# GpSimd subtracts for every second table, constants in the comparisons, and another order at the end, in an embedding lookup and MLP kernel

## The chip, the core and the metric

The kernel runs on one core of a Trainium2 chip. The core has a matrix engine (TensorE, PE in the profile, with its weight loads as PEld), three engines for elementwise work (VectorE = DVE, ScalarE = ACT, GpSimd = POOL) and SyncE (SP), which here only starts DMAs. They run side by side and wait for one another by semaphores. The metric is the device time of one execution, in microseconds (us), as a median over runs.

## What is computed

```python
e = stack([tbl_f[ids[:, f]] for f in range(32)], axis=1)      # (2048, 32, 64)
gram = einsum('bnd,bmd->bnm', e, e)
z = gram[:, rows, cols]                                        # 496 pairs above the diagonal
h = concatenate([z, dense_ctx], axis=1)                        # (2048, 512), dense_ctx has 16 columns
h = maximum(h @ W_top1 + b_top1, 0.0)                          # 512 -> 512
h = maximum(h @ W_top2 + b_top2, 0.0)                          # 512 -> 256
y = h @ W_top3                                                 # 256 -> 1
```

All is float32. 9 tables have 1000 rows, 8 have 1250, the rest 12500 or 125000.

## The kernel before

**Tiling.** The batch of 2048 is cut into eight super tiles of 256 examples (`SUPERS`, s = 0 to 7). The 17 smallest tables are `LOOKED_UP` (unit u = 0 to 16): their rows are not gathered but picked by matrix products. The other 15 tables are gathered by GpSimd with indirect DMAs (L264), two per table and super tile, so 30 in each super tile and 240 in all.

**A lookup by products.** A table lies in SBUF over 125 partitions, with 8 rows of it in each partition (1000 rows, u = 0 to 8) or 10 (1250 rows, u = 9 to 16); this number is `SPAN[u]`. VectorE makes one 0/1 matrix for each of the SPAN rows (`make_onehot`, L575): it compares `place`, the id of each example, spread over all partitions, with the partition's own code, a float32 per partition read from `codes_sb`. PE multiplies the 0/1 matrices with the table (`look_up`, L329), 2 x SPAN products for one unit. To keep float32's precision with bfloat16 products, each table is held in `split_sb` as three bfloat16 parts: high, middle and low.

**The head.** These parts are made once, while super tile 0 is looked up. For each unit ScalarE makes the high part (`high`, L504), VectorE subtracts it from the table (`take_high`, L605, into one of two `residue` buffers), ScalarE makes the middle part (`middle`, L508) and VectorE subtracts again to make the low part (`low`, L610). The semaphore `table_split` counts the low parts: PE waits for it ahead of each lookup of super tile 0, and `take_high` of the unit two further on waits for it because of the buffer. VectorE's order in the head is fixed in code: comparisons of u, `take_high(u+1)`, `low(u)`. The ids of super tiles 0 and 1 are spread over the partitions by PE in five pieces (`PIECES`, `spread_ids`, L315) and copied to `place` by ScalarE (`place_ids`, L476); those of later super tiles come by DMA. PE does a few products of no use before each lookup (`stay_warm`, L382). GpSimd does nothing but gathers: those of super tile 0 and then, when the index array has landed, those of super tile 1 and on; from super tile 2 on a gather waits for the drain that frees its rows.

**The middle.** In `step(s)` PE transposes the 32 fields in 8 groups (`transpose_group`, L299 and L302), computes the pair products (`gram_batch`, L346), and between these looks up super tile s+1 and does the MLP of s-1 (L358, L368, L375). The results of the pair products are folded by ScalarE (L463) and VectorE (L560) and laid out anew by 16 SBUF-to-SBUF DMAs (`move_cells`, L205); then 4 small DMAs write the 16 dense columns into `pairs` (L236), over cells that a move has written before.

**The end.** `step(7)` has nothing to look up. Its transposes go through four PSUM banks, drained by ScalarE and VectorE in turn (L441). Before its last group PE does 32 products of no use (`WARM_LAST`). Then come the pair products of s = 7, layers 1 to 3 of s = 6, and, once the 16 moves (10 from SP's queue, 6 from GpSimd's) and the 4 dense DMAs of s = 7 have landed, layers 1 to 3 of s = 7.

Of the kernel before, what the change touches and what calls it, by code (L numbers as in the profile page):

```python
# [9 lines left out]
P = 128  # L10
TILES = 2
# [5 lines left out]
WARM_FIRST, WARM_NEXT, WARM_LAST = 12, 4, 32  # L17
# [20 lines left out]
TP = 125  # L38
# [7 lines left out]
PIECES = [(0, 4), (4, 8), (8, 12), (12, 16), (16, 17)]  # L46
PIECE_OF = [p for p, (a, b) in enumerate(PIECES) for _ in range(a, b)]
assert len(PIECE_OF) == UNITS == FIRST_UNITS
# [8 lines left out]
READY_MADE = 3  # L57
assert READY_MADE < RING and READY_MADE <= UNITS
SP_MOVES = 10
# [34 lines left out]
def build(nc, ids, tables, dense, w1, b1, w2, b2, w3, identity, second, looked_ids, codes, out):  # L94
# [5 lines left out]
    with ctx:  # L100
# [44 lines left out]
        residue = [h1[0:TP].rearrange("p o b -> p (o b)"), pairs[0:TP, 0].rearrange("p i j q -> p (i j q)")]  # L145
# [24 lines left out]
        moved_by_pool = sem("moved_by_pool")  # L170
        dense_placed = [sem("dense_placed_even"), sem("dense_placed_odd")]
# [7 lines left out]
        whole_loaded = [sem(f"whole_loaded_{u}") for u in range(UNITS)]  # L179
        codes_loaded = sem("codes_loaded")  # L180
# [12 lines left out]
        table_split = sem("table_split")  # L193
# [13 lines left out]

        @block.sync
        def _(sp):
            sp.dma_start(index[:, 0], ids_v[0]).then_inc(first_index_loaded, 16)  # L210
            sp.dma_start(whole_ids, looked_ids).then_inc(whole_ids_loaded, 16)
            sp.dma_start(codes_sb[:], codes).then_inc(codes_loaded, 16)
# [9 lines left out]
            sp.dma_start(second_sb[:], second).then_inc(second_loaded, 16)  # L222
            for to, of in ((w1_sb, w1), (b1_sb, b1), (w2_sb, w2), (b2_sb, b2), (w3_sb, w3)):
                sp.dma_start(to[:], of).then_inc(weights_loaded, 16)

            def rearrange_pairs(s, parity, own=len(MOVES)):
# [5 lines left out]
                sp.wait_ge(pairs_moved, 16 * (len(MOVES) * s + own))  # L232
                if own < len(MOVES):
                    sp.wait_ge(moved_by_pool, 16 * (len(MOVES) - own))
# [432 lines left out]
```

## Time and profile before

| | us |
|---|---|
| median of 3 runs | 423.11 (422.06 to 423.18) |
| the profiled execution, its own time | 422.19 |
| its span in the trace | 420.4 |
| PE busy | 391.7 (93%) |
| VectorE busy | 297.6 (71%) |
| GpSimd busy | 249.3 (59%) |
| ScalarE busy | 168.9 (40%) |

All times in the trace count from the start of the span. The 1.8 us between the span and the execution's own time lie around the span and are not traced. A record's length is not the distance to the next one: VectorE's and PE's records overlap a little, so where a rate is wanted it is read from one start to the next. "Idle before" names what ended an engine's wait.

### The profile page before, as it was taken

The numbers are of one execution on the slowest core, as the hardware profiler recorded it, in microseconds if no ns is written. First come the engines' busy times: TensorE is split into PE (matmuls) and PEld (weight loads), VectorE is DVE, ScalarE is ACT, GpSimd is POOL, SyncE is SP. The second block draws the span as 40 slices with busy tenths as digits, with TensorE's granted clock in tenths as the row PEclk, the third lists the DMA queues.
The fourth block names the chain that finished last, engine by engine and source line by source line (L and its number), as shares of the span: only waits on it lengthen the run. The fifth ranks groups of instructions, "written<-read, shape, count | busy, mean of one in ns | idle before, by whom it ended". The sixth has DMA issues, their size and how long they took to land.

```text
span 420.4 us, 13473 instructions
## 1 busy us (share of the span) xinstructions
PE 391.7 (93%) x5554; PEld 357.0 (85%) x5554; DVE 297.6 (71%) x1295; ACT 168.9 (40%) x323; POOL 249.3 (59%) x250
## 2 busy tenths in 40 slices
PE   0876878999999999999999999999999999999987
PEld 0665668998999899988999899989999899989865
DVE  0799999998998379954998199846996389503200
ACT  2766743533533244323532354324532353222212
POOL 5777687777777777777777747774677700000200
PEclk9999999999999999999999999999999999999999
DMA  4445515212241342122511241132212200010100
GB/s 109 142 146 156 205 36 105 56 28 45 62 119 42 77 83 76 28 57 55 125 29 41 67 109 38 28 72 56 91 30 48 56 2 3 13 42 4 42 13 1
DMA packets 20991, 26.63 MB, mean 63 GB/s; under 512 B 9542, under 2 KB 13862, under 8 KB 20051
## 3 DMA queue, kind: packets, MB, share of 16 engines
q1 hardware_dynamic: 12882, 17.62, 12.5%
q0 software_dynamic: 7872, 8.08, 12.3%
q8 instruction: 44, 0.72, 0.8%
q14 instruction: 17, 0.14, 0.1%
q10 hardware_dynamic: 176, 0.08, 0.1%
HBM read 21.46 MB, written 0.08 MB: 51 GB/s over the span
## 4 chain that ended last, share of the span: by engine, by line
PE 81%; DVE 10%; DMA 3%; SPq 2%; issue 2%; ACT 2%; DVEq 0%
PE turn_ps L329 43%; PE mlp_ps L358 12%; PE gram_ps L346 8%; DVE onehot L575 6%; PE mlp_ps L368 6%; PE mlp_ps L299 5%; PE mlp_ps L302 3%; DVE split_sb L610 3%; PE mlp_ps L375 2%; DMA id_row<-half_ids 1%; SPq L205 1%; PE gram_ps L382 1%; ACT place L476 1%; PE mlp_ps L382 1%; DMA index<-looked_ids 1%
## 5 line engine op out<-in xcount | busy, mean ns | idle before, releaser
L264 POOL DMA_INDIRECT rows<-tbl,index x240 | 246.1, 1026 | 88.5 <-issue 71.6
L575 DVE TENSOR_SCALAR onehot<-place,codes_sb 125x256 bf16<-125x256 f16 x1216 | 250.9, 297 | 8.4 <-PE turn_ps L329 5.0
L329 PE MATMUL turn_ps<-split_sb,onehot 125*128 125x192 bf16 x2432 | 219.0, 246 | 10.7 <-DVE split_sb L610 10.7
L329 PEld LDWEIGHTS turn_ps<-split_sb,onehot 125*128 125x128 bf16 x2432 | 199.7, 98 | 17.2 <-DVE split_sb L610 14.0
L470 ACT CAST parts<-turn_ps 128x384 bf16<-128x384 f32 x136 | 65.2, 480 | 125.3 <-PE turn_ps L329 123.8
L553 DVE COPY y_room<-mlp_ps 1x256 f32<-1x256 f32 x8 | 5.0, 627 | 78.8 <-PE mlp_ps L375 78.8
L358 PE MATMUL mlp_ps<-pairs,w_sb 128*128 128x256 f32 x256 | 56.9, 380 | 1.0 <-DMA pairs<-dense 1.0
L358 PEld LDWEIGHTS mlp_ps<-pairs,w_sb 128*128 128x128 f32 x256 | 48.0, 190 | 7.8 <-DMA pairs<-dense 1.5
L441 ACT COPY emb_t<-mlp_ps 128x512 f32<-128x512 f32 x58 | 34.0, 586 | 14.3 <-PE mlp_ps L299 13.4
L346 PE MATMUL gram_ps<-emb_t 64*64 64x64 f32 x2048 | 37.5, 221 | 1.2 <-DVE folded L560 0.7
L346 PEld LDWEIGHTS gram_ps<-emb_t 64*64 64x64 f32 x2048 | 33.3, 134 | 6.1 <-issue 6.1
L205 POOL DMA_DIRECT2D pairs<-folded x6 | 3.0, 520 | 59.3 <-DVE folded L560 59.3
L560 DVE COPY_PREDICATED folded<-second_sb,gram_ps 128x512 f32<-128x512 int32 x32 | 23.1, 721 | 19.3 <-ACT folded L463 19.3
L458 ACT ACTIVATE h<-mlp_ps,b_sb 128x256 f32<-128x256 f32 x32 | 13.4, 471 | 47.5 <-PE mlp_ps L358 41.5
L463 ACT COPY folded<-gram_ps 128x512 f32<-128x512 f32 x32 | 18.8, 586 | 28.7 <-PE gram_ps L346 27.4
L299 PE MATMUL mlp_ps<-ident_bf,parts 128*128 128x128 bf16 x384 | 27.7, 219 | 1.4 <-ACT ident_bf L533 0.8
L368 PE MATMUL mlp_ps<-h,w_sb 128*128 128x256 f32 x128 | 28.9, 379 | 0.0
L299 PEld LDWEIGHTS mlp_ps<-ident_bf,parts 128*128 128x128 bf16 x384 | 23.5, 98 | 4.6 <-ACT parts L470 2.6
L368 PEld LDWEIGHTS mlp_ps<-h,w_sb 128*128 128x128 f32 x128 | 23.9, 190 | 3.7
L315 PE MATMUL gram_ps<-id_row,ones 1*125 1x512 f16 (+1 forms) x18 | 7.3, 508 | 10.7 <-DMA id_row<-half_ids 9.6
L302 PE MATMUL mlp_ps<-ident_sb,rows 128*128 128x128 f32 x112 | 17.1, 272 | 0.0
L482 ACT ACTIVATE h<-mlp_ps,b_sb 128x256 f32<-128x256 f32 x16 | 6.7, 471 | 20.9 <-PE mlp_ps L368 20.9
(37 smaller groups left out, 123.6 us busy)
## 6 DMA issues: line engine op xcount, KB each, us to landing
place<-ids_scratch SPq DMA_DIRECT2D x6, 1062.5 KB
pairs<-folded SPq DMA_DIRECT2D x122, 32.0 KB
rows<-tbl,index POOLq DMA_INDIRECT x240, 3.8
emb_t<-tbl SPq DMA_DIRECT2D x8, 250.0 KB
folded<-tbl SPq DMA_DIRECT2D x5, 312.5 KB
w_sb<-w SPq DMA_DIRECT2D x1, 1024.0 KB
y_room<-tbl SPq DMA_DIRECT2D x3, 312.5 KB
w_sb<-w SPq DMA_DIRECT2D x1, 512.0 KB
```

The lines of the kernel that those rows point to most:

```text
L264: nc.gpsimd.indirect_dma_start(rows[:, s % 2, slot - UNITS, t, :], None, tables[f][:, :], bass.IndirectOffsetOnAxis(index[:, s, t, f:f + 1 ...
L299: last = nc.tensor.matmul(turn_bank[g % banks][:, k, :], parts[:, slot, a].rearrange("p t d -> p (t d)"), ident_bf[:], start=(a == 0), sto ...
L302: last = nc.tensor.transpose(turn_bank[g % banks][:, k, :], rows[:, parity, slot - UNITS].rearrange("p t d -> p (t d)"), ident_sb[:])
L329: last = nc.tensor.matmul(turn_ps[:, n % 2].rearrange("p k b -> p (k b)")[:, t * PARTS * DIM:(t + 1) * PARTS * DIM], onehot[:, n % RING, c ...
L346: last = nc.tensor.matmul(gram_ps[FIELDS * i:FIELDS * (i + SIDE), k % 2, t, u].rearrange("p h ij -> p (h ij)"), e.rearrange("p b f -> p (b ...
L358: last = nc.tensor.matmul(mlp_ps[:, o // 2, o % 2, :], w1_sb[:, jj, P * o:P * (o + 1)], pairs[:, parity, :, jj, :], start=(jj == 0), stop= ...
L368: last = nc.tensor.matmul(mlp_ps[:, 0, o, :], w2_sb[:, k, P * o:P * (o + 1)], h1[:, k, :], start=(k == 0), stop=(k == OT1 - 1))
L441: copy(emb_t[:, :, GROUP_F * g:GROUP_F * (g + 1)], turn_bank[g % banks].rearrange("p f b -> p b f")).then_inc(done, 1)
L463: nc.scalar.copy(folded[:, parity, :, :, BATCH_Q * k:BATCH_Q * (k + 1)].rearrange("p i j (q t) -> p (i j) q t", t=TILES), gram_ps[:, k % 2 ...
L470: nc.scalar.copy(parts[:, u], turn_ps[:, n % 2].rearrange("p k b -> p (k b)")[:, 0:TILES * PARTS * DIM] .rearrange("p (t a d) -> p a t d", ...
L560: nc.vector.copy_predicated(folded[:, parity, :, :, BATCH_Q * k:BATCH_Q * (k + 1)].rearrange("p i j (q t) -> p (i j) q t", t=TILES), secon ...
L575: last = nc.vector.tensor_scalar(onehot[:, n % RING, c, :], place[:, parity, u, :], codes_sb[:, CODE_AT[SPAN[u]] + c:CODE_AT[SPAN[u]] + c ...
```

## The change

1. **Head, low parts.** `low(u)` of even u (0, 2, ... 16: nine units) is issued by GpSimd instead of VectorE, in its queue behind gathers 9, 12, 15, ... 33, counted from 0 (`LOW_BEHIND`). `table_split` becomes two semaphores, for even and for odd units. A third residue buffer is added, so `take_high(u)` waits for the low part of u-3 instead of u-2.
2. **Comparisons.** For s = 0 and 1 the code is a constant in the instruction instead of a float32 per partition from `codes_sb`. For this `place_ids` subtracts SPAN x partition from the ids by a per-partition bias (`shift_sb`, a new small DMA ahead of those of codes, identity and tables), and `PIECES` is cut so that no piece mixes the two spans.
3. **End.** The four tiles of layer 1 of s = 6 are issued before the last transpose group in the place of the 32 warm products. The transposes of `step(7)` use two banks instead of four (the other two now belong to layer 1). The 16 moves of s = 7 are issued 6 by SP, 5 by ScalarE and 5 by GpSimd. The dense columns of s = 7 are loaded early into `last_dense` (1 mask DMA and 4 data DMAs on SP, ahead of the weights) and put in place by one masked VectorE copy of 1024 elements per partition, in the place of the 4 DMAs behind the moves.

```diff
-PIECES = [(0, 4), (4, 8), (8, 12), (12, 16), (16, 17)]
+PIECES = [(0, 4), (4, 8), (8, 9), (9, 13), (13, 17)]
+LOW_BEHIND = [9 + 3 * n for n in range((UNITS + 1) // 2)]
-SP_MOVES = 10
+SP_MOVES, ACT_MOVES = 6, 5
...
         @block.gpsimd
         def _(pool):
+            def low(u):
+                pool.wait_ge(middle_split, u + 1)
+                nc.gpsimd.tensor_tensor(part(u, 2), table_rows(u, residue[u % len(residue)]), part(u, 1),
+                                        ALU.subtract).then_inc(table_split[0], 1)
...
                         ).then_inc(rows_landed[s % 2][slot // GROUP_F], 16)
+                        made = (FIELDS - UNITS) * TILES * s + TILES * (slot - UNITS) + t
+                        if made in LOW_BEHIND:
+                            low(2 * LOW_BEHIND.index(made))
...
                 if first:
-                    pe.wait_ge(table_split, u + 1)
+                    pe.wait_ge(table_split[u % 2], u // 2 + 1)
...
                     if not ahead and g == GROUPS - 1:
+                        for o in range(OT1):
+                            layer1_tile(s - 1, o, 1 - parity, turn - 1 + parity)
                         pe.wait_ge(second_copied, GRAM_EMPTY + GRAM_BATCHES * s)
-                        stay_warm(WARM_LAST, last_warm)
-                    transpose_group(s, parity, turn, g, 2 if ahead else 4)
+                    transpose_group(s, parity, turn, g, turn_bank if ahead else last_bank)
...
-                nc.scalar.copy(place[:, s, a:b, :].rearrange("p u q -> p (u q)"),
-                               gram_flat[0:TP, piece % 2, 0:SUPER * (b - a)]).then_inc(placed, 1)
+                nc.scalar.activation(place[:, s, a:b, :].rearrange("p u q -> p (u q)"),
+                                     gram_flat[0:TP, piece % 2, 0:SUPER * (b - a)], ACT.Identity,
+                                     bias=shift_sb[:, piece:piece + 1]).then_inc(placed, 1)
...
                     last = nc.vector.tensor_scalar(onehot[:, n % RING, c, :], place[:, parity, u, :],
-                                                   codes_sb[:, CODE_AT[SPAN[u]] + c:CODE_AT[SPAN[u]] + c + 1], None, ALU.is_equal)
+                                                   codes_sb[:, CODE_AT[SPAN[u]] + c:CODE_AT[SPAN[u]] + c + 1]
+                                                   if s > 1 else float(c), None, ALU.is_equal)
...
             def take_high(u):
-                if u >= 2:
-                    dve.wait_ge(table_split, u - 1)
+                if u >= len(residue):
+                    v = u - len(residue)
+                    dve.wait_ge(table_split[v % 2], v // 2 + 1)
...
                 if u + 1 < UNITS:
                     take_high(u + 1)
-                low(u)
+                if u % 2:
+                    low(u)
...
+            nc.vector.copy_predicated(pairs[:, 1].rearrange("p i j q -> p j i q"),
+                                      dense_mask[:].unsqueeze(2).unsqueeze(2).to_broadcast([P, CHUNKS, QUAD, QUADS]),
+                                      last_dense[:].unsqueeze(1).to_broadcast([P, CHUNKS, QUAD, QUADS])
+                                      ).then_inc(last_dense_placed, 1)
             layer3_drain(SUPERS - 2)
             layer3_drain(SUPERS - 1)
```

GpSimd's queue before, whole: the gathers follow one another without anything between them.

```order
6 L264 DMA rows<-tbl,index 128x64 x240
7 L205 DMA pairs<-folded 32x256 x6
8 L100 UNCONDITIONAL_BRANCH
```

GpSimd's queue now, the head part of it: ten gathers, then an instruction named ISA that the kernel's code does not ask for (the build puts it in front of the first subtraction), then nine subtractions with three gathers between each two.

```order
6 L293 DMA rows<-tbl,index 128x64 x10
7 L284 ISA
8 L284 TENSOR_TENSOR split_sb<-h,split_sb 125x8x64
9 L293 DMA rows<-tbl,index 128x64 x3
10 L284 TENSOR_TENSOR split_sb<-pairs,split_sb 125x8x64
11 L293 DMA rows<-tbl,index 128x64 x3
...
24 L284 TENSOR_TENSOR split_sb<-pairs,split_sb 125x10x64
25 L293 DMA rows<-tbl,index 128x64 x206
```

So every low part of an even unit now stands behind that ISA instruction and behind the gathers ahead of it.

PE at the end, before (L382 are the products of no use, L346 the pair products, L358, L368 and L375 the layers 1 to 3, first of s = 6, then of s = 7):

```order
244 L302 MATMUL mlp_ps<-ident_sb,rows 128x128 x7
245 L302 MATMUL turn_ps<-ident_sb,rows 128x128 x4
246 L382 MATMUL gram_ps<-ident_sb 128x128 x32
247 L302 MATMUL turn_ps<-ident_sb,rows 128x128 x4
248 L382 MATMUL gram_ps<-ident_sb 128x128 x4
249 L346 MATMUL gram_ps<-emb_t 64x64 x128
250 L358 MATMUL mlp_ps<-pairs,w_sb 128x256 x16
251 L368 MATMUL mlp_ps<-h,w_sb 128x256 x8
252 L375 MATMUL mlp_ps<-h,w_sb 1x256 x2
253 L358 MATMUL mlp_ps<-pairs,w_sb 128x256 x16
```

PE at the end, now (the same functions stand at L334, L416, L378, L392, L402 and L409):

```order
243 L334 MATMUL turn_ps<-ident_sb,rows 128x128 x11
244 L392 MATMUL mlp_ps<-pairs,w_sb 128x256 x16
245 L334 MATMUL turn_ps<-ident_sb,rows 128x128 x4
246 L416 MATMUL gram_ps<-ident_sb 128x128 x4
247 L378 MATMUL gram_ps<-emb_t 64x64 x128
248 L402 MATMUL mlp_ps<-h,w_sb 128x256 x8
249 L409 MATMUL mlp_ps<-h,w_sb 1x256 x2
250 L392 MATMUL mlp_ps<-pairs,w_sb 128x256 x16
```

Layer 1 of s = 6 has moved from behind the pair products to before the last transpose group, where the 32 products of no use were.

## Rows read from the trace of the kernel before

**Rows 1.** The page's chain that ended last, by engine:
```profile
PE 81%; DVE 10%; DMA 3%; SPq 2%; issue 2%; ACT 2%; DVEq 0%
```
**Rows 2.** Windows (us, busy us of each engine, granted clock): head, step 0, end:
```profile
18.00:65.00 47.00, 36.29 (x359) 30.51 (x358) 46.09 (x165) 29.30 (x50) 35.31 (x31) 1.00 0.41 132
65.00:111.00 46.00, 44.57 (x762) 43.20 (x761) 44.18 (x208) 19.60 (x39) 35.02 (x37) 1.00 0.29 62
```
**Rows 3.** Timeline (start, us) of one unit in the head, all engines:
```profile
57.09 0.81 DVE L605 TENSOR_TENSOR pairs<-y_room,split_sb 125x640 f32<-125x640 f32 x1
57.58 1.88 POOL L264 DMA_INDIRECT rows<-tbl,index  x1 [0.30 <-issue]
57.83 0.81 DVE L610 TENSOR_TENSOR split_sb<-h,split_sb 125x640 bf16<-125x640 f32 x1
58.56 2.20 DVE L575 TENSOR_SCALAR onehot<-place,codes_sb 125x256 bf16<-125x256 f16 x10
58.70 1.82 PE L329 MATMUL turn_ps<-split_sb,onehot 125*128 125x192 bf16 x20 [1.17 <-DVE split_sb L610]
59.77 0.94 POOL L264 DMA_INDIRECT rows<-tbl,index  x1 [0.30 <-issue]
60.36 0.60 PE L382 MATMUL mlp_ps<-ident_sb 128*128 128x128 f32 x4
60.53 0.81 DVE L605 TENSOR_TENSOR h<-y_room,split_sb 125x640 f32<-125x640 f32 x1
```
**Rows 4.** Timeline: the first lookup, the longest gather and gather 10, the last lookup:
```profile
13.21 2.27 POOL L264 DMA_INDIRECT rows<-tbl,index  x1 [0.30 <-issue]
17.03 1.23 POOL L264 DMA_INDIRECT rows<-tbl,index  x1 [0.30 <-issue]
17.69 1.77 PE L329 MATMUL turn_ps<-split_sb,onehot 125*128 125x192 bf16 x16
...
64.84 1.82 PE L329 MATMUL turn_ps<-split_sb,onehot 125*128 125x192 bf16 x20 [0.44 <-DVE split_sb L610]
```
**Rows 5.** Groups by shape (busy us, mean ns of one): ScalarE's copies, a subtraction:
```profile
L470 ACT CAST parts<-turn_ps 128x384 bf16<-128x384 f32 x136 | 65.2, 480 | 125.3 <-PE turn_ps L329 123.8 <-issue 1.5
L441 ACT COPY emb_t<-mlp_ps 128x512 f32<-128x512 f32 x58 | 34.0, 586 | 14.3 <-PE mlp_ps L299 13.4 <-PE mlp_ps L302 0.6 <-issue 0.2
L458 ACT ACTIVATE h<-mlp_ps,b_sb 128x256 f32<-128x256 f32 x32 | 13.4, 471 | 47.5 <-PE mlp_ps L358 41.5 <-issue 6.0
L610 DVE TENSOR_TENSOR split_sb<-h,split_sb 125x512 bf16<-125x512 f32 x5 | 3.4, 682 | 0.9 <-ACT split_sb L508 0.9
L511 ACT ACT_TABLE_LOAD x1 | 1.3, 1283 | 0.8 <-PEq L637 0.8
```
**Rows 6.** The comparisons' line: duration in ns, min/median/max, first and last start:
```profile
L575 DVE TENSOR_SCALAR onehot<-place,codes_sb x1216: 246/280/524, 11.8 to 362.2; 125x256 bf16<-125x256 f16 x174
```
**Rows 7.** DMA issues: KB each, us from issue to landing:
```profile
ids_scratch<-half_ids ACTq DMA_DIRECT2D x1, 68.0 KB, 5.7
id_row<-half_ids SPq DMA_DIRECT2D x1, 8.5 KB, 13.5
```
**Rows 8.** Groups in the window 13 to 66 us, GpSimd alone:
```profile
L264 POOL DMA_INDIRECT rows<-tbl,index x34 | 41.0, 1207 | 12.9 <-issue 10.1 <-DMA index<-ids 2.9
```
**Rows 9.** Timeline of the end:
```profile
382.40 3.66 PE L382 MATMUL gram_ps<-ident_sb 128*128 128x128 f32 x32
...
392.51 7.17 PE L358 MATMUL mlp_ps<-pairs,w_sb 128*128 128x256 f32 x32
...
393.34 0.73 DVE L560 COPY_PREDICATED folded<-second_sb,gram_ps 128x512 f32<-128x512 int32 x1 [0.20 <-ACT folded L463]
394.10 6.28 SPq L205 DMA_DIRECT2D pairs<-folded  x10
...
401.69 2.78 SPq L236 DMA_DIRECT2D pairs<-dense  x4
...
405.71 7.17 PE L358 MATMUL mlp_ps<-pairs,w_sb 128*128 128x256 f32 x32 [0.99 <-DMA pairs<-dense]
```

More of the change, by code:

```diff
@@ L16 @@
 QUADS = SUPER // QUAD
[L17 removed]
+WARM_FIRST, WARM_NEXT = 12, 4
 SIDE = 2
@@ L44 @@
 RING = 4
-PIECES = [(0, 4), (4, 8), (8, 12), (12, 16), (16, 17)]
+PIECES = [(0, 4), (4, 8), (8, 9), (9, 13), (13, 17)]
 PIECE_OF = [p for p, (a, b) in enumerate(PIECES) for _ in range(a, b)]
-assert len(PIECE_OF) == UNITS == FIRST_UNITS
+assert len(PIECE_OF) == UNITS == FIRST_UNITS and all(len(set(SPAN[a:b])) == 1 for a, b in PIECES)
 SPANS = sorted(set(SPAN))
@@ L91, in slot_meaning, with build @@
     return rows, np.tile(second, (QUAD, SIDE))
-def build(nc, ids, tables, dense, w1, b1, w2, b2, w3, identity, second, looked_ids, codes, out):
+def build(nc, ids, tables, dense, w1, b1, w2, b2, w3, identity, second, dense_cells, looked_ids, codes, shift, out):
     fp32, i32, bf16, fp16 = mybir.dt.float32, mybir.dt.int32, mybir.dt.bfloat16, mybir.dt.float16
@@ L206, in move_cells, with part, table_rows @@
                                     folded[FIELDS * i:FIELDS * (i + 1), parity, i % SIDE, CHUNKS * jq:CHUNKS * (jq + 1), :])
+        def part(u, which):
+            return split_sb[:, SPAN_AT[u]:SPAN_AT[u + 1], which, :]
+        def table_rows(u, flat):
+            return flat[:, 0:SPAN[u] * DIM].rearrange("p (c d) -> p c d", d=DIM)
         @block.sync
@@ L230, in rearrange_pairs @@
                     move_cells(sp, i, jq, parity).then_inc(pairs_moved, 16)
-                sp.wait_ge(pairs_moved, 16 * (len(MOVES) * s + own))
-                if own < len(MOVES):
-                    sp.wait_ge(moved_by_pool, 16 * (len(MOVES) - own))
+                if not place_dense:
+                    return
+                sp.wait_ge(pairs_moved, 16 * len(MOVES) * (s + 1))
                 for jj in range(CHUNKS):
@@ L441, in drain_turned @@
             copy(emb_t[:, :, GROUP_F * g:GROUP_F * (g + 1)],
-                 turn_bank[g % banks].rearrange("p f b -> p b f")).then_inc(done, 1)
-        def part(u, which):
-            return split_sb[:, SPAN_AT[u]:SPAN_AT[u + 1], which, :]
-        def table_rows(u, flat):
-            return flat[:, 0:SPAN[u] * DIM].rearrange("p (c d) -> p c d", d=DIM)
+                 banks[g % 2].rearrange("p f b -> p b f")).then_inc(done, 1)
         @block.scalar
@@ L489, in step @@
                             keep_parts(s + 1, u)
-                    drain_turned(act, nc.scalar.copy, turned_drained, s, g, 2 if ahead else 4)
+                    drain_turned(act, nc.scalar.copy, turned_drained, s, g, turn_bank if ahead else last_bank)
+                if not ahead:
+                    layer1_half(s - 1, 0)
+                    layer1_half(s - 1, 1)
                 for k in range(SLOTS):
@@ L507, in middle @@
                 act.wait_ge(high_taken, u + 1)
-                nc.scalar.copy(part(u, 1), table_rows(u, residue[u % 2])).then_inc(middle_split, 1)
+                nc.scalar.copy(part(u, 1), table_rows(u, residue[u % len(residue)])).then_inc(middle_split, 1)
             act.wait_ge(whole_ids_loaded, 16)
@@ L664 @@
     out = nc.dram_tensor("out", (BATCH, 1), mybir.dt.float32, kind="ExternalOutput").ap()
-    build(nc, ids, tables, dense, w1, b1, w2, b2, w3, identity, second, looked_ids, codes, out)
+    build(nc, ids, tables, dense, w1, b1, w2, b2, w3, identity, second, dense_cells, looked_ids, codes, shift, out)
     return run_bass_kernel_spmd(nc, [arrays], core_ids=[0]).results[0]["out"]
```

84 lines of the change are left out of this document (58 added, 26 removed).

## The prediction

> **What bounds the kernel now.** I read the chain that ended last first: 81% of it is PE, 10% VectorE [rows 1]. The windows say where VectorE's part lies. In the head (18 to 65 us) VectorE is busy 46.09 of 47 us and PE 36.29; in step 0 PE is busy 44.57 of 46 [rows 2], and from there to the last super tile PE has no gap worth naming. The granted clock is 1.00 in both stretches [rows 2], the upper level of 2.4 GHz. So time can come from two places: the head, which VectorE sets, and the end, where PE waits for the dense DMAs. In the head the timeline of one unit shows the pace [rows 3]: from `take_high` at 57.09 to the next at 60.53 is 3.44 us, made of two subtractions (57.09, 57.83, 58.56: 0.74 us each) and ten comparisons (58.56 to 60.53: 0.197 each). PE waits 1.17 us for the low part in each such unit. The first lookup runs at 17.69, the last at 64.84 [rows 4]: the head is these 47.2 us.
>
> **The comparisons (part 2).** In the head 9 x 8 + 8 x 10 = 152 comparisons lose their per-partition scalar. What that is worth no row shows; it is bounded from both sides. A subtraction of 512 elements takes 682 ns [rows 5] and one of 640 takes 0.81 us [rows 3]: about 1.02 ns per element, so some 0.16 us of a record are fixed. A comparison of 256 elements takes 280 ns in the median [rows 6]. If it streams two elements per such step, it takes 0.13 + 0.16 = 0.29 and the scalar costs nothing: the one end, 0. If it streams four, 0.065 + 0.16 = 0.225 and the scalar costs about 0.06. ScalarE is the other end: its copies of 384 and 512 elements take 480 and 586 ns, so one of 256 would take 374, and an activation of 256 with a per-partition bias takes 471 [rows 5], 0.10 us more. I take 0.06, the value that VectorE's own rows give if the scalar costs anything. That makes a comparison 0.14 and VectorE's head shorter by 152 x 0.06 = 9.1 us, if nothing else comes late. In step 0 the same saving falls beside a busy PE [rows 2] and is worth nothing. `place_ids` pays ScalarE's 0.1 us ten times, on an engine that is busy 29 of 47 us [rows 2].
>
> **The low parts (part 1).** VectorE gives up nine subtractions, five of 0.60 us (from start to start, 512 elements) and four of 0.74: 5.9 us. GpSimd gets them, and there they stand in one queue with the gathers. Three costs follow.
>
> First, the ISA instruction that the order shows between gather 9 and the first subtraction. No row of the trace has one. Its lower end is 0. It brings something in that this engine did not need before, so the nearest rows are those of loads: ScalarE's table load takes 1.28 us [rows 5], a DMA of 68 KB issued at 4.79 us on a queue of its own, with the table loads under way, lands after 5.7 us, and one queued behind the tables after 13.5, the upper end [rows 7]. I take a fetch and an installation, 5.7 + 1.3 = 7.0 us. The Trainium skill ("GPSIMD Engine Reference", § 2.1 Instruction dispatch) says that the first call to a freshly loaded GpSimd kernel pays about 6 us that the profile does not show as an instruction; no run here shows it yet. By that figure the sum below would be 1 us less, and it speaks against this change as a whole.
>
> Second, a subtraction on GpSimd. Lower end: VectorE's 0.68 us [rows 5]; upper end: the longest thing that GpSimd does in the head, a gather of 2.27 us [rows 4]. I take 1.2 for 512 elements and 1.4 for 640, in the lower half, since it moves two streams as VectorE does but in software. The same page (§ 3) gives 4497 ns for 2048 elements, in proportion an estimate of 1.1 and 1.4.
>
> Third, the pace of the queue. A gather takes 0.94 us and 0.30 of issue ahead of it [rows 3], 1.24 in all, but it is stretched while VectorE subtracts: 1.88 us for the one that meets two subtractions [rows 3]. Over the head 34 gathers average 1.207 us [rows 8], 0.267 more than 0.94, together 9.1 us for 33 subtractions, 0.28 each.
>
> Now the head after the change. Gather 10 began at 17.03 [rows 4]; in its place stands the ISA instruction, until 24.0. `low(0)` is done at 25.3 and PE looks unit 0 up at 25.4 instead of 17.7. VectorE meanwhile prepares units 1 to 3 and stops at `take_high(3)`, which waits for that low part. From `low(0)` to `low(16)` GpSimd has to do 24 gathers (24 x 1.24 = 29.8), eight subtractions with their waits (4 x 1.3 + 4 x 1.5 = 11.2) and the stretching by the 21 subtractions that VectorE has left (21 x 0.28 = 5.9): 46.9 us. The others are faster. VectorE has 128 comparisons (17.9), 14 `take_high` and 7 `low` (14.3) left, 32 us. PE's records are 1.77 us for 16 products, 1.82 for 20 and 0.60 for four warm ones [rows 3, 4]; they overlap, so 9 x 2.37 + 8 x 2.42 = 40.7 us and some 3 for the id pieces are more than it needs. So GpSimd sets the pace of the head and the 9.1 us of the comparisons are covered by its queue. The last lookup comes at 25.4 + 46.9 = 72.3 instead of 64.84: **+7.4 us**. What waits behind GpSimd's waits: gathers 10 to 29 of super tile 0, needed by step 0's transposes some 10 us after the head, and the index load, for which gather 30 waits 2.9 us now [rows 8], is by then long there; both are hidden.
>
> **The end (part 3).** Before, from the last fold (393.34 + 0.73 = 394.07) to layer 1 of s = 7 at 405.71 there are 11.6 us: ten issues in 6.28, 1.3 to landing, four dense issues in 2.78 from 401.69, and 1.2 to landing [rows 9]. Now: six issues at 0.63 (3.8), landing 1.3, the masked copy. This one has 1024 elements per partition; the fold does 512 in 0.73 [rows 9], so its bounds are 0.73 and 1.46, and with 512 x 1.02 ns more I take 1.25. With 0.15 for the handovers that is 6.5: -5.1 us. ScalarE's and GpSimd's five issues each take less than SP's six. Layer 2 and 3 of s = 6 (3.6 + 1.0 and ScalarE's work behind its five issues) end some 2 us before that and are hidden. Against it stand two costs ahead of the pair products. Layer 1 (7.17 for its 32 records) takes the place of the warm products (3.66) [rows 9]: +3.5. With two banks a transpose group waits for the drain of the one two before it: 0.73 of transposes, 0.59 of ScalarE's copy [rows 5] and some 0.2 of handover per two groups, where four banks let PE run on: about +0.8 by the seventh group. Sum: **-0.8 us**. The five early dense and mask DMAs and the shift DMA cost 0.4 to 0.6 us of SP's time each, ahead of tables and weights; the only table that is waited for is the first, and 0.4 us there disappears in the wait for the ISA instruction.
>
> **Sum.** +7.4 - 0.8 = +6.6 us on the profiled execution's 422.19: 428.8. That execution lies 0.9 below the median of three runs, so I say 429.0. About 1.3 us (0.3%) is what a measurement here can tell from no change.
>
> **The rivals.**
> - *The ISA instruction is free or nearly* (chance 0.24). For it: no trace shows a price, and something may be resident. Then `low(0)` is done at 18.3, just behind PE's readiness at 17.7, GpSimd's 46.9 us end at 65.3 (+0.5), and the end gives 0.8: 421.9. This is the other side: its price decides, and the sign turns at about 0.3 us. With shorter subtractions or less stretching (5 us at most) this goes down to 417.
> - *GpSimd keeps up* (0.08). The load costs 7 us, but gathers are not stretched as before, because VectorE subtracts less densely; VectorE or PE then sets the pace. GpSimd without stretching needs 41 us: last lookup at 66.4, +1.6 - 0.8, so 423.0.
> - *The scalar costs nothing* (0.09). VectorE then needs 25.2 + 14.3 = 39.5 us after `low(0)`, which alone is still hidden. But if a subtraction on GpSimd keeps VectorE from working for its whole length, 10.4 us more come on top, and 50 us are more than GpSimd's 46.9: +3.1, so 432. The Trainium skill ("SBUF — State Buffer", § Who interferes with whom) says just this of the shared port pair, an exclusive lock that fully blocks the loser; in the trace a gather is stretched by subtractions [rows 3], while VectorE shows no such loss to gathers.
> - *The end turns round* (0.07). If SP's and ScalarE's issues share one generator, 11 issues at 0.63 take 6.9 instead of 3.8: +3.1, so 432.
> - The forecast itself, 425 to 431.5 with the load between 4 and 9.5 us: 0.52.
>
> That the comparisons or moves are not changed as described is excluded by the order of instructions. Whether PE's clock falls in the 7.7 us without a lookup no row shows; the first lookups would be slower for it, behind GpSimd's queue, and I add nothing.
>
> **Numbers.** Range 420.5 to 433.5: it holds the forecast's cases, the middle of the free-load case and both dear ones. Faster by over 0.3%: 0.13 of the first rival and 0.01 of the second, 0.14. Within 0.3%: 0.09 + 0.03, 0.12. Slower: 0.74.
>
> **What the profile after would show.** The first lookup (L361) near 25.4 us instead of 17.7, with a gap on GpSimd of about 7 us after its tenth gather: the load. The last one near 72. PE in the head waiting for GpSimd's `split_sb` of even units, not for VectorE; VectorE waiting in `take_high`; comparisons 0.14 us apart there and 0.20 later. GpSimd's subtractions at 1.2 and 1.4 us. From the last fold to the last layer 1, 6.5 us instead of 11.6, and 4.3 us more between the last lookup of s = 7 and the pair products. I am wrong if GpSimd shows no gap, if even units' low parts are ready before PE asks, or if layer 1 of s = 7 waits for moves issued by ScalarE.

## The result, and the profile after

The changed kernel takes **432.1 us** (median of 427.8 to 433.2), the one before 422.7 beside it: a ratio of 1.0205 [1.0128, 1.0281], 9.4 us slower. The profiled execution takes 433.18 us with a span of 431.4, against 422.19 and 420.4.

Where its 11.0 us lie, from one start to the next: the last lookup of the head begins at 73.40 instead of 64.84 [rows 4], **+8.56**. From there to the first transposes of s = 7 (386.82) there are 313.42 us, before 313.37: the middle is as it was. From there to the end of the last product (428.91) there are 42.09, before 39.71 (378.21 to 417.92): **+2.38**.

Windows of the kernel after (us, busy us of each engine, granted clock), against [rows 2]:

```profile
18.00:40.00 22.00, 17.22 (x172) 15.46 (x172) 19.91 (x70) 12.41 (x24) 17.51 (x17) 1.00 0.44 146
40.00:60.00 20.00, 16.56 (x128) 13.09 (x126) 16.11 (x68) 13.15 (x21) 14.92 (x10) 0.83 0.44 136
60.00:75.00 15.00, 9.21 (x85) 8.71 (x82) 8.27 (x47) 3.73 (x7) 12.14 (x7) 0.77 0.29 72
```

VectorE, which was idle for only 0.9 of 47 us in the head, now is for a fifth of 40 to 60 us and for almost half of 60 to 75, and PE's granted clock, 1.00 everywhere before, is 0.83 and 0.77.

GpSimd around its first subtraction, and the first lookup (timeline of after: start, duration), against [rows 4]:

```profile
14.39 0.94 POOL L293 DMA_INDIRECT rows<-tbl,index  x1 [0.31 <-issue]
15.43 1.18 POOL L284 TENSOR_TENSOR split_sb<-h,split_sb 125x512 bf16<-125x512 f32 x1
18.21 2.43 PE L361 MATMUL turn_ps<-split_sb,onehot 125*128 125x192 bf16 x16
```

The gather ends at 15.33, the subtraction starts 0.10 us later: the ISA instruction between them costs nothing that can be seen.

The other places, in order of time:

```profile
26.59 2.70 DVE L613 TENSOR_SCALAR onehot<-place 125x256 bf16<-125x256 f16 x8
26.91 1.16 POOL L284 TENSOR_TENSOR split_sb<-pairs,split_sb 125x512 bf16<-125x512 f32 x1
...
42.68 1.43 DVE L613 TENSOR_SCALAR onehot<-place 125x256 bf16<-125x256 f16 x10
43.24 4.95 POOL L284 TENSOR_TENSOR split_sb<-pairs,split_sb 125x640 bf16<-125x640 f32 x1 [1.27 <-ACT split_sb L542]
44.03 0.81 DVE L645 TENSOR_TENSOR pairs<-folded,split_sb 125x640 f32<-125x640 f32 x1
44.77 1.43 DVE L613 TENSOR_SCALAR onehot<-place 125x256 bf16<-125x256 f16 x10
46.12 0.81 DVE L645 TENSOR_TENSOR h<-folded,split_sb 125x640 f32<-125x640 f32 x1
47.00 1.87 DVE L650 TENSOR_TENSOR split_sb<-pairs,split_sb 125x640 bf16<-125x640 f32 x1
48.24 3.38 PE L361 MATMUL turn_ps<-split_sb,onehot 125*128 125x192 bf16 x20 [2.45 <-POOL split_sb L284]
...
60.60 6.57 POOL L284 TENSOR_TENSOR split_sb<-pairs,split_sb 125x640 bf16<-125x640 f32 x1 [1.97 <-ACT split_sb L542]
63.40 2.52 DVE L613 TENSOR_SCALAR onehot<-place 125x256 bf16<-125x256 f16 x18
67.23 3.38 PE L361 MATMUL turn_ps<-split_sb,onehot 125*128 125x192 bf16 x20 [5.79 <-POOL split_sb L284]
...
73.40 1.82 PE L361 MATMUL turn_ps<-split_sb,onehot 125*128 125x192 bf16 x20
```

Three things stand there. At 26.6 eight comparisons take 2.70 us where they take 1.26 when GpSimd doesn't subtract: they stood still for its 1.16 us and some. At 43.24 and 60.60 it is the other way round: the record of a 1.4 us subtraction lasts 4.95 and 6.57 us. Each record began while VectorE had instruction behind instruction ready, and ended 1.26 us after VectorE's first pause (46.93 to 47.00) and 1.25 us after VectorE had nothing left at all (63.40 + 2.52 = 65.92). And PE, which had waited for it, then takes 3.38 us for 20 products instead of 1.82: the granted clock over these two records is 0.50, the lower of its two levels (1.2 instead of 2.4 GHz).

The end (timeline of after), against [rows 9]:

```profile
407.23 4.08 SPq L216 DMA_DIRECT2D pairs<-folded  x6
407.24 3.14 ACTq L216 DMA_DIRECT2D pairs<-folded  x5
407.51 2.54 POOL L216 DMA_DIRECT2D pairs<-folded  x5 [64.54 <-DVE folded L598]
412.63 1.29 DVE L675 COPY_PREDICATED pairs<-dense_mask,last_dense 128x1024 f32<-128x1024 int32 x1 [5.43 <-DMA pairs<-folded]
413.98 9.89 PE L392 MATMUL mlp_ps<-pairs,w_sb 128*128 128x256 f32 x32 [2.01 <-DVE pairs L675]
```

Layer 1 of s = 7 begins 6.8 us after the last fold (407.20) instead of 11.6, but takes 9.89 us instead of 7.17, at a granted clock of 0.72 instead of 1.00 (the first row is after, the second before):

```profile
413.98:423.87 9.89, 9.89 (x33) 8.29 (x34) 0.45 (x1) 0.84 (x2) 0.00 (x0) 0.72 0.01 2
405.71:412.88 7.17, 7.17 (x33) 6.34 (x34) 0.00 (x0) 0.84 (x2) 0.00 (x0) 1.00 0.00 0
```

One thing is needed to read the experiments: they ran on three chips, and on two of these (all runs but g4 and g5) every kernel, the one before too, took 669 to 704 us, because from some point in or behind the head PE issued single products, mostly 1 to 3 us apart, for a reason that I haven't found; there the ratios say nothing sure of the change, but the head up to that point, and the end, whose undisturbed records agree with those above, can be read.

### The profile page after: what moved, and what is told of

It is laid out like the page before. It is cut to its first block, busy times and chain, and to the rows that moved or that the text cites. A ratio compares the mean times of both kernels' runs of the same rounds, so it can differ in the third digit from the quotient of the medians.

```text
span 431.4 us, 13416 instructions
## 1 busy us (share of the span) xinstructions
PE 396.4 (92%) x5522; PEld 360.4 (84%) x5522; DVE 286.2 (66%) x1288; ACT 168.7 (39%) x323; POOL 262.2 (61%) x258
## 4 chain that ended last, share of the span: by engine, by line
PE 85%; DVE 4%; ACT 4%; POOL 3%; DMA 2%; issue 1%; SPq 1%; DVEq 0%; ACTq 0%
PE turn_ps L361 45%; PE mlp_ps L392 14%; PE gram_ps L378 8%; PE mlp_ps L402 6%; PE mlp_ps L331 5%; PE mlp_ps L334 3%; POOL split_sb L284 3%; DVE onehot L613 2%; PE mlp_ps L409 2%; PE mlp_ps L416 1%; ACT place L506 1%; DMA id_row<-half_ids 1%; PE gram_ps L347 1%; ACT split_sb L542 1%; SPq L216 1%
## 5 line engine op out<-in xcount | busy, mean ns | idle before, releaser
L293 POOL DMA_INDIRECT rows<-tbl,index x240 | 239.3, 997 | 76.7 <-issue 70.6
L361 PE MATMUL turn_ps<-split_sb,onehot 125*128 125x192 bf16 x2432 | 223.4, 249 | 14.0 <-POOL split_sb L284 9.6
L361 PEld LDWEIGHTS turn_ps<-split_sb,onehot 125*128 125x128 bf16 x2432 | 204.0, 99 | 20.1 <-POOL split_sb L284 12.9
L613 DVE TENSOR_SCALAR onehot<-place,codes_sb 125x256 bf16<-125x256 f16 x912 | 187.8, 295 | 5.5 <-PE turn_ps L361 4.9
L613 DVE TENSOR_SCALAR onehot<-place 125x256 bf16<-125x256 f16 x304 | 52.8, 257 | 15.0 <-PE turn_ps L361 12.1
L392 PE MATMUL mlp_ps<-pairs,w_sb 128*128 128x256 f32 x256 | 59.6, 393 | 2.0 <-DVE pairs L675 2.0
L392 PEld LDWEIGHTS mlp_ps<-pairs,w_sb 128*128 128x128 f32 x256 | 50.0, 198 | 9.5 <-DVE pairs L675 2.5
L378 PE MATMUL gram_ps<-emb_t 64*64 64x64 f32 x2048 | 37.5, 221 | 1.5 <-issue 0.7
L378 PEld LDWEIGHTS gram_ps<-emb_t 64*64 64x64 f32 x2048 | 33.3, 134 | 6.3 <-issue 6.3
L488 ACT ACTIVATE h<-mlp_ps,b_sb 128x256 f32<-128x256 f32 x32 | 13.4, 470 | 51.0 <-PE mlp_ps L392 45.4
L402 PE MATMUL mlp_ps<-h,w_sb 128*128 128x256 f32 x128 | 29.0, 380 | 0.0
L331 PE MATMUL mlp_ps<-ident_bf,parts 128*128 128x128 bf16 x357 | 25.8, 219 | 1.4 <-ACT ident_bf L568 0.8
L402 PEld LDWEIGHTS mlp_ps<-h,w_sb 128*128 128x128 f32 x128 | 23.9, 190 | 3.7
L284 POOL TENSOR_TENSOR split_sb<-pairs,split_sb 125x512 bf16<-125x512 f32 (+1 forms) x6 | 16.4, 2734 | 5.7 <-ACT split_sb L542 5.6
```

Of the source, the lines that this page charges most:

```text
L284: nc.gpsimd.tensor_tensor(part(u, 2), table_rows(u, residue[u % len(residue)]), part(u, 1), ALU.subtract).then_inc(table_split[0], 1)
L293: nc.gpsimd.indirect_dma_start(rows[:, s % 2, slot - UNITS, t, :], None, tables[f][:, :], bass.IndirectOffsetOnAxis(index[:, s, t, f:f + 1 ...
L331: last = nc.tensor.matmul(banks[g % 2][:, k, :], parts[:, slot, a].rearrange("p t d -> p (t d)"), ident_bf[:], start=(a == 0), stop=(a == ...
L361: last = nc.tensor.matmul(turn_ps[:, n % 2].rearrange("p k b -> p (k b)")[:, t * PARTS * DIM:(t + 1) * PARTS * DIM], onehot[:, n % RING, c ...
L378: last = nc.tensor.matmul(gram_ps[FIELDS * i:FIELDS * (i + SIDE), k % 2, t, u].rearrange("p h ij -> p (h ij)"), e.rearrange("p b f -> p (b ...
L392: last = nc.tensor.matmul(mlp_ps[:, o // 2, o % 2, :], w1_sb[:, jj, P * o:P * (o + 1)], pairs[:, parity, :, jj, :], start=(jj == 0), stop= ...
```

## The experiments

**First: is GpSimd's part the loss?** g4 is the changed kernel with all low parts back on VectorE (parts 2 and 3 of the change).

```diff
-                        if made in LOW_BEHIND:
-                            low(2 * LOW_BEHIND.index(made))
...
-                                        ALU.subtract).then_inc(table_split[1], 1)
+                                        ALU.subtract).then_inc(table_split[u % 2], 1)
...
-                if u % 2:
-                    low(u)
+                low(u)
```

> The changed kernel with every low part back on VectorE (parts 2 and 3 of the change alone). Theory (what is lost is lost where GpSimd's subtractions and VectorE shut each other out, and in the clock behind PE's waits): VectorE's head is shorter by the comparisons' 8 to 9 us, the last lookup of the head at 57 us or so, the granted clock of the head 1.00, the pair products' clock at the end as in the changed kernel: 416 to 419 us against 423 before. Rival (the loss lies at the end, or in the immediates and the id copies): 426 us or more.

Measured: **418.2 us against 422.5**, ratio 0.9894 [0.9863, 0.9925]. Three of the four runs took 417.9 to 418.3 us; the fourth took 430.5, at a mean granted clock of 0.984 instead of 0.996, and isn't in the ratio. No trace of it was kept, so why this kernel can also take nearly as long as the changed one is open. The last lookup of the head:

```profile
57.90 1.82 PE L358 MATMUL turn_ps<-split_sb,onehot 125*128 125x192 bf16 x20 [0.56 <-DVE split_sb L647]
59.98 1.60 PEld L358 LDWEIGHTS turn_ps<-split_sb,onehot 125*128 125x128 bf16 x20
60.00 1.81 PE L358 MATMUL turn_ps<-split_sb,onehot 125*128 125x192 bf16 x20
```

60.00 instead of 64.84 (57 was expected), the granted clock 1.00 from 18 to 60 us. So the nine subtractions on GpSimd cost about 14 us (432.1 against 418.2, in separate comparisons whose kernels before agree within 0.2 us). The saving of the comparisons is 4.8 us of the head and not 9.1; three rows of g4 say why (timeline: a unit of 10, a unit of 8, the wait of the third unit):

```profile
54.94 1.43 DVE L610 TENSOR_SCALAR onehot<-place 125x256 bf16<-125x256 f16 x10
27.59 1.32 DVE L610 TENSOR_SCALAR onehot<-place 125x256 bf16<-125x256 f16 x8
22.03 0.69 DVE L647 TENSOR_TENSOR split_sb<-pairs,split_sb 125x512 bf16<-125x512 f32 x1 [2.67 <-ACT split_sb L539]
```

Ten comparisons take 1.36 us from their start to the next start (54.94 to 56.30) while GpSimd does nothing beside them, 0.136 each: 0.61 us less per unit, 4.9 in eight units, as foreseen. The units of 8 run beside gathers: theirs take 0.156 each, and with a subtraction that takes 0.73 instead of 0.68 the unit gets only 0.27 us shorter (2.51 instead of 2.78), 2.4 in nine. Of the 7.3 us, 0.4 go in VectorE's first comparisons (12.21 instead of 11.80) and 1.8 in its wait at 22.03 (2.67 us, before 0.91). That wait is for ScalarE, which is behind the copy of the first lookup's results, and this lookup starts at 18.29 instead of 17.69 and takes 2.68 us instead of 1.77. Why it is late and slow no run isolates. The rest, some 0.3 us, is unaccounted for.

GpSimd does nothing there because of this row of g4:

```profile
48.71 16.37 POOL L293 DMA_INDIRECT rows<-tbl,index  x1 [7.11 <-DMA index<-ids]
59.86 4.41 DVE L610 TENSOR_SCALAR onehot<-place 125x256 bf16<-125x256 f16 x32
```

A gather of 0.94 us lasts from 48.71 to 65.08, 0.81 us beyond the end of VectorE's work without a pause (59.86 + 4.41 = 64.27). It is kept out like the subtractions in the changed kernel, without any of them in the queue; PE never waits for gathered rows in this trace. In e4, the same kernel, VectorE has no pause until 82.83 + 4.42 = 87.25, and a gather lasts from 51.14 to 88.07, again 0.82 us more:

```profile
51.14 36.93 POOL L293 DMA_INDIRECT rows<-tbl,index  x1 [0.30 <-issue]
82.83 4.42 DVE L610 TENSOR_SCALAR onehot<-place 125x256 bf16<-125x256 f16 x32
```

**Part 1 alone**, on two chips: GpSimd subtracts, but the comparisons keep their per-partition scalar and the end is the old one. From the edit against the kernel before:

```diff
+                        if made in LOW_BEHIND:
+                            low(2 * LOW_BEHIND.index(made))
...
-                low(u)
+                if u % 2:
+                    low(u)
```

> The kernel before with part 1 alone: even units' low parts on GpSimd, comparisons still with a scalar per partition (0.20 us apart), the old end. Theory A (the two engines exclude each other; a subtraction on GpSimd either holds VectorE up for its 1.2 to 1.4 us or waits until VectorE pauses): VectorE gains 0.60 to 0.74 us for each low part and loses 1.2 to 1.4, so the head gets 4 to 6 us longer even if no subtraction waits long; with one or two that wait 4 us or more it is 427 to 431 us. Theory B (GpSimd's queue with its gathers sets the pace, no exclusion): the last lookup near 65, 422 to 424 us, no GpSimd subtraction above 2 us and no comparison group stretched.

> Part 1 alone again (even units' low parts on GpSimd, comparisons still with a scalar per partition, 0.20 us apart). Theory A (exclusion, and a wait for a pause only when VectorE's comparisons come 0.14 us apart): all nine subtractions take 1.15 to 1.45 us, each holds a group of comparisons or a subtraction of VectorE up by about as much, so the head gets 4 to 6 us longer: 427. Theory A' (a subtraction on GpSimd can also wait long behind comparisons 0.20 us apart): one or two of 4 us or more. Theory B (no exclusion): 422 to 424.

Total times 677 and 678 us where the kernel before takes 694 and 691 (e2: ratio 0.9791 [0.9718, 0.9864]). This is no gain of part 1 that can be told from the disturbance: in the three kernels with GpSimd's subtractions (e2, f2, f5) PE's row of single products begins at 76 to 78 us, in those without at 22 to 29, and whether the kernel or chance makes that difference is open. The head is undisturbed up to 74 us but for one gap of 0.67 us (e2, at 43.04), at a granted clock of 1.00. Its last lookup begins at 68.60 and 69.65: **+3.8 and +4.8 us** against before. Timeline of e2, VectorE and GpSimd:

```profile
50.40 3.25 DVE L585 TENSOR_SCALAR onehot<-place,codes_sb 125x256 bf16<-125x256 f16 x10
51.73 1.44 POOL L268 TENSOR_TENSOR split_sb<-h,split_sb 125x640 bf16<-125x640 f32 x1 [2.63 <-ACT split_sb L518]
54.31 2.05 DVE L585 TENSOR_SCALAR onehot<-place,codes_sb 125x256 bf16<-125x256 f16 x10
57.75 3.22 DVE L585 TENSOR_SCALAR onehot<-place,codes_sb 125x256 bf16<-125x256 f16 x10
58.31 1.40 POOL L268 TENSOR_TENSOR split_sb<-pairs,split_sb 125x640 bf16<-125x640 f32 x1 [1.46 <-ACT split_sb L518]
```

Ten comparisons take 2.05 us, and 3.2 when a GpSimd subtraction falls into them: VectorE loses 1.2 us to each, and is spared 0.60 to 0.74. Nine times that difference is 4 to 5 us, which is the whole +3.8 to +4.8. Part 1 makes the engine that sets the head slower, not faster, even if nothing else goes wrong. None of the 18 subtractions in the two traces takes over 1.63 us: Theory A' finds nothing here.

**Can GpSimd be kept from waiting?** g5 is the changed kernel, in which VectorE pauses for GpSimd's low part.

```diff
                 if u % 2:
                     low(u)
+                else:
+                    dve.wait_ge(table_split[0], u // 2 + 1)
```

> The changed kernel, in which VectorE, having taken the high part of unit u + 1, waits until GpSimd has made the low part of an even unit u. Theory (back to back comparisons on VectorE keep GpSimd's subtraction out until VectorE pauses): none of the nine subtractions is over 2 us, where the changed kernel has one of 4.95 and one of 6.57; PE's waits of 2.45 and 5.79 us for them go, the clock of the head stays at 1.00, and the last lookup comes at 66 to 70 us instead of 73.4: 425 to 429 us against 432. Rival (the queue of gathers alone sets when the low parts are made): the waits make VectorE later still, 432 to 436 us.

Measured: **425.0 us against 422.5**, ratio 1.0069 [1.0042, 1.0097], so 7 us less than the changed kernel by giving VectorE more to wait for. The last lookup comes at 65.83, the granted clock of the head is 1.00, and PE's longest wait for GpSimd is 1.08 us. The expectation missed in one point: two subtractions are still over 2 us (2.86 and 2.69), since they wait as long as VectorE has work, which is now the rest of a group of comparisons and one `take_high`:

```profile
55.72 1.43 DVE L613 TENSOR_SCALAR onehot<-place 125x256 bf16<-125x256 f16 x10
56.45 2.69 POOL L284 TENSOR_TENSOR split_sb<-pairs,split_sb 125x640 bf16<-125x640 f32 x1 [1.57 <-ACT split_sb L542]
57.08 0.81 DVE L645 TENSOR_TENSOR h<-y_room,split_sb 125x640 f32<-125x640 f32 x1
59.18 1.64 DVE L613 TENSOR_SCALAR onehot<-place 125x256 bf16<-125x256 f16 x10 [1.29 <-POOL split_sb L284]
59.20 1.82 PE L361 MATMUL turn_ps<-split_sb,onehot 125*128 125x192 bf16 x20 [1.08 <-POOL split_sb L284]
```

The same kernel on a chip that disturbs it:

> The changed kernel with one wait added on VectorE: after take_high(u+1) of even u it waits for the low part of u from GpSimd, so it stands still while GpSimd subtracts. Theory A (long GpSimd subtractions are waits for a pause of VectorE): no GpSimd subtraction above 1.45 us, no comparison group stretched to 2.7 us, PE never waits more than about 2 us in the head, its clock stays 1.00; the time falls to 424 to 427 although a wait was added, and the runs agree better. Theory B (they are long for another reason, as a slow memory or GpSimd's own work): two of 5 us or more remain, 432 us or above.

678.8 us (before 691), not usable. Its nine subtractions take 1.15 to 1.86 us; the one of 60.59 that came out of a wait met VectorE at the end of its last instruction (59.82 + 0.82). Of Theory A three signs failed: two subtractions took over 1.45 us (1.86 and 1.85), PE waited 3.00 us for GpSimd at 36.73, and the granted clock over the 16 products behind that wait was 0.58. The cause lies in GpSimd's queue, where a gather at 30.97 took 3.28 us, until 0.81 us after VectorE's pause at 33.44, and the low part stood behind it. A pause of VectorE for the low part doesn't keep the gathers ahead of it from being shut out.

Which instruction is kept out and which gets in can be put in numbers only. In the ten traces with constants in the comparisons there are ten records of GpSimd in the head over 2.5 us: four subtractions (4.95 and 6.57 in after, 2.86 and 2.69 in g5) and six gathers (16.37 in g4, 36.93 in e4, 25.24 in f4, and three of 3.3 in f1 and f5). Nine of the ten end 1.25 to 1.26 us (subtractions) or 0.81 to 0.82 us (gathers) after VectorE's first pause; the tenth, f1's second gather (50.13 to 53.41), ends while VectorE has none. In the four traces with the scalar per partition (before, e2, f2, e3) the longest is 2.27. That points to comparisons with a constant, which follow one another at 0.14 us instead of 0.20, as what leaves GpSimd little room; but three traces with constants (e1, h1, h2) have no such record, so what decides it in one case stays open.

**The end.** e3 is part 3 alone (with the third residue buffer, all low parts on VectorE); h1 is g4 with products of no use in PE's two pauses at the end.

```diff
             layer2(SUPERS - 2)
+            pe.wait_ge(second_copied, GRAM_EMPTY + GRAM_BATCHES * SUPERS)
+            stay_warm(12, last_warm)
             layer3(SUPERS - 2)
+            stay_warm(16, last_warm)
```

> The kernel before with part 3 alone (and the third residue buffer, with all low parts on VectorE): new end, old head. Theory A (the end's own balance is -0.3 us, and PE's clock falls in the gap before layer 1 of s = 7): layer 1 of s = 7 starts 27.2 us after the first transpose group of s = 7 instead of 27.5, its 32 records take 9.9 us instead of 7.17 at a granted clock near 0.8; 425 us. Theory B (the clock fell only because the head had already had gaps in this run, or by chance): 7.2 us for layer 1, 422.4 us.

> Parts 2 and 3 without the GpSimd subtractions, and with 12 warm products between layers 2 and 3 of super tile 6 and 16 between its layer 3 and layer 1 of super tile 7, where PE otherwise waits 1.6 and 2.0 us. Theory (the granted clock falls behind PE's pauses at the end): layer 1 of super tile 7 takes about 7.2 us for its 32 products instead of 8.8, and the time is 416.5 us against 418.2 without the products. Rival (the clock falls for another reason, layer 1's own weight loads for one): 8.8 us again, and 418 us or more.

Totals of 701.2 (before 694.2) and 693.9 (before 693.2), not usable. The end itself is. In e3 layer 1 of s = 7 starts 26.6 us after the first transposes (27.2 expected, before 27.5) and takes 8.66 us (9.9 expected): Theory A in kind. PE's last products in e3, then in h1:

```profile
673.74 3.72 PE L396 MATMUL mlp_ps<-h,w_sb 128*128 128x256 f32 x16
679.04 1.02 PE L403 MATMUL mlp_ps<-h,w_sb 128*1 128x256 f32 x4 [1.58 <-ACT h L506]
682.09 8.66 PE L386 MATMUL mlp_ps<-pairs,w_sb 128*128 128x256 f32 x32 [2.02 <-DVE pairs L665]
690.58 3.62 PE L396 MATMUL mlp_ps<-h,w_sb 128*128 128x256 f32 x16
```

```profile
671.69 1.47 PE L413 MATMUL gram_ps<-ident_sb 128*128 128x128 f32 x12
673.44 1.02 PE L406 MATMUL mlp_ps<-h,w_sb 128*1 128x256 f32 x4 [0.28 <-ACT h L513]
674.39 1.97 PE L413 MATMUL gram_ps<-ident_sb 128*128 128x128 f32 x16
676.51 7.17 PE L389 MATMUL mlp_ps<-pairs,w_sb 128*128 128x256 f32 x32
683.52 3.62 PE L399 MATMUL mlp_ps<-h,w_sb 128*128 128x256 f32 x16
```

Over all traces:

| end | traces | first transposes of s = 7 to last product | layer 1 of s = 7 |
|---|---|---|---|
| old | 6 | 39.45 to 40.04 us (before: 39.71) | 7.17 in all |
| new | 7 | 40.29 to 42.31 us (after: 42.09) | 8.64 to 10.12 |
| new, pauses filled (h1) | 1 | 38.83 us | 7.17 |

With PE's pauses of 1.6 and 2.0 us filled, layer 1 is back at 7.17 us and the new end is 0.9 us shorter than the old. The granted clock over layer 1 is 1.00 in h1, 0.82 in e3 and 0.81 in g4. So the rearranged end gains up to what its steps say (layer 1 starts 0.9 us earlier than before in e3, g4, g5 and h1, 0.7 in f5, but only 0.3 in after, e4 and f4, which no run explains; among the old ends it varies by 0.6), and PE's clock, which falls behind the pauses, takes 1.5 to 3 us for it. That h1's variant would run at about 416.6 us (g4's 418.2 less 1.6) is an estimate; no run of it on a chip that doesn't disturb it exists.

**Part 2 alone, and parts 2 and 3**, on the disturbing chips.

> The kernel before with part 2 alone: constants in the comparisons of s = 0 and 1 (with the shifted ids and the new pieces), nothing on GpSimd, the old end. Theory: VectorE sets the head, so the 152 cheaper comparisons (0.06 us each, 9.1 us) move the last lookup of the head from 64.84 us to about 58, where PE's own pace begins to bind; 422.7 - 7 = 416 us. Rival (what the prediction's third rival says, that the scalar costs nothing): comparisons stay 0.20 us apart, 422 to 423 us.

> Part 2 alone again (constants in the comparisons of s = 0 and 1), since the first comparison ran on a chip on which every kernel, the one before too, took some 690 us. Theory: the last lookup of the head moves from 64.84 us to about 58 and the time falls by 7 us, to 416; the comparisons stand 0.14 us apart. Rival: the scalar costs nothing or the saving is hidden, 422 to 423.

> Part 2 alone (immediates and relative ids), the end and the low parts as before. Theory (the rearranged end gains 0.8 us in its steps and gives 1.6 us back in the slower clock of the last layer 1): about 1 us less than parts 2 and 3 together, 417 us, with layer 1 of super tile 7 at 7.2 us. Rival (the end is worth what its steps say): 419 us.

> The changed kernel with all low parts given back to VectorE: parts 2 and 3 without part 1. If the low parts on GpSimd are what made the change slower, the last lookup of the head is near 58 us instead of 73.4, PE's clock stays 1.00 in the head, and the time is the sum of the two runs before it: about 416 to 419 us, 13 to 16 us below the changed kernel. If the head's loss came from something else in the change, it stays above 425 us.

> Parts 2 and 3 without part 1: the changed kernel with all low parts given back to VectorE. If GpSimd's subtractions made the change slower, the last lookup of the head is near 58 us instead of 73.4 and the clock is 1.00 through the head. At the end, with a head without gaps: if PE's clock falls by the gap ahead of layer 1 of s = 7, its records take 9 to 10 us and the time is 417 to 418; if it doesn't fall, 7.2 us and 415 to 416.

693.2, 687.3 and 693.9 us for part 2 alone, 695.0 and 694.6 for parts 2 and 3, all within their own scatter of the kernel before there (694.2, 690.9, 693.2). They decide nothing about the times, nor about the last lookup that they were to show: PE's single products begin at 22 to 28 us, as this row of e1 shows:

```profile
35.41 0.32 PE L332 MATMUL turn_ps<-split_sb,onehot 125*128 125x192 bf16 x1 [2.48 <-issue]
```

What they do show: eight comparisons with a constant take 1.16 to 1.33 us there (1.65 with the scalar), and the old end belongs to a layer 1 of 7.17 us. Whether part 2 alone beats parts 2 and 3 remains open.

## Why the prediction was right in its number and wrong in its reason

**Right.** Slower, 429.0 against 432.1, inside the range of 420.5 to 433.5. That the number came so near is luck: in the head +7.4 us stands against +8.6, and not one of its two terms was what happened. (The forecast's own terms, +6.6 on the median of 423.11, give 429.7, not 429.0.) The comparisons' price (0.20 to 0.14 us) holds. A subtraction on GpSimd takes 1.16 to 1.18 and 1.40 us where it doesn't wait, as taken. The end: 6.8 us from last fold to layer 1 (6.5 foreseen), the masked copy 1.29 (1.25), 4.3 us more before the pair products (4.3). h1 puts the whole at -0.9 us where the sum had -0.8; in the changed kernel itself layer 1 of s = 7 starts 0.3 us earlier, 27.16 us after the first transposes instead of 27.50.

**Wrong: the ISA instruction as a load of 7.0 us.** It costs 0.1 us at most, and the first lookup comes at 18.2, not 25.4. That is the prediction's own first sign of being wrong: GpSimd shows no gap. The Trainium skill ("GPSIMD Engine Reference", § 2.1) names some 6 us for the first call to a freshly loaded kernel, which this trace doesn't show; taking the nearest rows of loads as the value, rather than as an upper end, was the mis-step. With that alone the rival "free or nearly" should have come true, 421.9. It did not, since two other steps were wrong as well.

**Wrong: "GpSimd sets the pace of the head", 46.9 us from `low(0)` to `low(16)`.** GpSimd isn't short of time: in five of nine cases it waits for ScalarE's middle part (0.6 to 2.0 us each). Of the 56.4 us from its first subtraction (15.43) to its last (71.83), 6.2 are such waits and 8.7 the excess of the two long records over 1.4 us. VectorE never waits for a low part of GpSimd's in `take_high`, as it should have. So the comparisons' 9.1 us weren't covered by its queue either: without the subtractions on GpSimd (g4) 4.8 of them reach the end of the head.

**Missing: that a GpSimd subtraction and VectorE's work exclude each other.** The prediction had this only in the rival "the scalar costs nothing" (10.4 us of standing still), and hung it on a condition that it doesn't need. A group of comparisons into which a subtraction falls takes 1.2 to 1.6 us longer, with either kind of operand. Nor does VectorE lose nothing to gathers, as the prediction read it: with constants a comparison takes 0.156 us beside gathers and 0.136 without (g4). The Trainium skill ("SBUF — State Buffer", § Who interferes with whom) has the rule: the one that issues first keeps the pair for its instruction, the other blocks. The traces agree as to the standing still; they differ in that GpSimd waited at 43.24 through the rest of a group of comparisons, two subtractions and ten more comparisons, and at 60.60 through all that VectorE had, not for one instruction. Where no subtraction waits long, part 1 costs 4 to 5 us (e2, f2); the long waits and what follows from them cost the rest: 73.4 instead of some 64 us, which is what the parts alone add up to (64.84 - 4.8 + 4.3).

**Missing: the clock.** "I add nothing" was 3.8 us too little in the head's records (3.38, 2.51 and 3.38 us instead of 1.82), besides a first lookup of 2.43 us instead of 1.77, and the end has no term for the clock at all, where 2.7 us are lost (9.89 against 7.17). In the head it feeds back: ScalarE copies PE's results ahead of the next middle part, and VectorE waits for that (after):

```profile
55.41 0.48 ACT L500 CAST parts<-turn_ps 128x384 bf16<-128x384 f32 x1 [1.64 <-PE turn_ps L361]
56.99 0.71 ACT L542 CAST split_sb<-pairs 125x640 bf16<-125x640 f32 x1
57.74 0.82 DVE L650 TENSOR_TENSOR split_sb<-pairs,split_sb 125x640 bf16<-125x640 f32 x1 [2.44 <-ACT split_sb L542]
```

Put by its own terms, the +7.4 of the head was a load (0 in fact) and a queue (not binding); the +8.6 measured is standing still (+4.3), long waits with the slower clock behind them (+9, which is what is left of the 8.6 and not measured by itself), less the comparisons (-4.8).

## What to carry to other kernels

Work moved from VectorE to GpSimd did not run beside VectorE in this kernel, whose two engines both work in SBUF: price it as what VectorE stands still (here 1.2 us or more for 0.6 to 0.74 us saved), and if the moved piece is on the path, let VectorE pause for it rather than run ahead, since GpSimd may not get in before VectorE pauses (425.0 us with the pauses, 432.1 without). Of a bundle of three edits two can be good and the bundle bad; taking the one out gave 418.2 us, the best kernel measured, though one of its four runs took 430.5. Where a wait on PE becomes shorter by rearranging, look at the pauses that are left: filling them with products of no use kept the clock up for the layer behind them.

## What the runs showed of the hardware

- GpSimd can be kept out for long: a subtraction of 1.40 us had a record of 6.57 us and a gather of 0.94 us one of 16.37, and both ended about one duration of their own (1.25 and 0.81 us) after VectorE's first pause. Of the ten records over 2.5 us nine ended so, one without a pause (f1).
- The reverse: a group of comparisons of 1.26 us takes 2.70 when a subtraction of 1.16 us runs (constants, after), and one of 2.05 takes 3.25 with a subtraction of 1.44 us (scalar per partition, e2).
- A scalar per partition instead of a constant costs VectorE 0.06 us in a comparison of 256 elements (2.05 against 1.43 us for ten).
- The clock fell behind pauses of PE of 2.45 and 5.79 us in the head (after) and of 3.00 us (f5), and behind pauses of 1.6 and 2.0 us with 1 us of four small products between at the end (seven traces), while the old end's pauses of 0.6 and 1.0 to 1.2 us left it at 7.17 us for layer 1 (six traces).
